# Second layer's expansion in a graph network: two engines evict, rings of eight groups, four pairs of PSUM banks

## The reference

```python
feat_n = feat * jax.lax.rsqrt(out_deg)[:, None]
h_src = feat_n[src]
copy_sum = jax.ops.segment_sum(h_src, dst, num_segments=N)
inner_sum = jax.ops.segment_sum(h_src * feat_n[dst], dst, num_segments=N)
rst = copy_sum @ weight1 + inner_sum @ weight2
...
rst = rst * jax.lax.rsqrt(in_deg)[:, None]
```

## Time and profile before

| | us |
|---|---|
| median of 3 runs | 19314.47 |
| lowest, highest run | 19310.16, 19331.81 |
| span of the profiled execution | 19335.7 |
| the expansion `ex2` in it, 13010 to 13755 | 745.0 |

### The profile page before, as it was taken

One profiled execution on the slowest core, in us unless ns is written; L12 is line 12 of the kernel. 1 busy time (PEld: TensorE's weight loads), 2 busy tenths in 40 slices (PEclk: granted clock), 3 DMA queues, 4 the chain that ended last, 5 costly groups with the idle time before them and its releaser, 6 DMA issues. The chain is left out here.

```text
span 19335.7 us, 330621 instructions
## 1 busy us (share of the span) xinstructions
PE 11298.7 (58%) x72558; PEld 8581.2 (44%) x72559; DVE 10446.0 (54%) x36907; ACT 4413.4 (23%) x11783; POOL 8860.6 (46%) x9490
## 2 busy tenths in 40 slices
PE   5555555555545666564475666656555665446886
PEld 4333333333324555554375444433224553225776
DVE  7655555555542333333464777772345445777776
ACT  0011111111101222221011342006201112445665
POOL 0456556556551555555674344530362444333332
PEclk9766766667665666666555566765555555557887
DMA  7622222222222222223233798757543776665554
GB/s 313 253 63 65 63 64 63 62 65 63 65 59 69 58 57 57 57 57 56 50 58 33 249 312 271 214 169 241 174 127 89 228 224 213 216 216 175 174 173 142
DMA packets 2143987, 2588.95 MB, mean 134 GB/s; under 512 B 892151, under 2 KB 1761472, under 8 KB 2143848
## 3 DMA queue, kind: packets, MB, share of 16 engines
q1 hardware_dynamic: 1755208, 1752.17, 31.5%
q0 software_dynamic: 353792, 654.90, 11.6%
q10 hardware_dynamic: 34848, 180.49, 2.3%
HBM read 1738.16 MB, written 848.30 MB: 134 GB/s over the span
## 5 line engine op out<-in xcount | busy, mean ns | idle before, releaser
L556 POOL DMA_INDIRECT edges_by_dst<-rec,pos x1568 | 1527.2, 974 | 2135.3 <-DVE rec L491 1694.2
L989 POOL DMA_INDIRECT sc_rows<-src_table,sc_idx x1664 | 1581.9, 951 | 1484.8 <-DVE sc_tp L1087 813.7
L556 POOL DMA_INDIRECT edges_by_cell<-rec,pos x1568 | 1532.7, 977 | 528.7 <-issue 528.4
L1734 PE MATMUL ex_rows<-table,ex_oh 128*128 x6528 | 1173.5, 348 | 821.1 <-DVE ex_oh L1702 423.8
L1820 PE MATMUL gs_part<-gs_rows,gs_oh 128*128 128x192 bf16 x6528 | 1100.8, 332 | 787.6 <-DVE gs_oh L1793 309.3
L1039 PE MATMUL sc_loc<-dst_table,sc_ohT 128*128 x3328 | 767.1, 403 | 1140.3 <-ACT sc_ohT L1005 1097.2
L1782 POOL DMA_INDIRECT gs_rows<-rows_by_src,chunk_read_by_src x1088 | 1059.9, 974 | 778.2 <-PE gs_part L1820 474.6
L2221 PE MATMUL at_part<-cell_edge_term,key_in_block 128*66 128x128 f32 x8704 | 1218.1, 304 | 252.4 <-issue 201.2
L1734 PEld LDWEIGHTS ex_rows<-table,ex_oh 128*128 128x128 bf16 x6528 | 752.1, 132 | 1242.2 <-issue 1202.7
L520 DVE SCALAR_TENSOR_TENSOR junk<-rowb,keycol,earlier 128x128 f32<-128x128 f32 (+1 forms) x3136 | 1151.4, 413 | 240.5 <-issue 236.3
L2221 PEld LDWEIGHTS at_part<-cell_edge_term,key_in_block 128*66 128x66 f32 x8704 | 1132.0, 158 | 323.5 <-issue 302.9
(11 more groups left out here) (393 smaller groups left out, 25910.8 us busy)
## 6 DMA issues: line engine op xcount, KB each, us to landing
ex_keys<-src_key_rows SPq DMA_DIRECT2D x1632, 128.0 KB
rows_by_src<-ex_stage SPq DMA_DIRECT2D x1088, 192.0 KB
rowb<-sort_key_rows SPq DMA_DIRECT2D x392, 512.0 KB
ex_keys<-dst_key_rows SPq DMA_DIRECT2D x1088, 128.0 KB
dst_rows_by_src<-patY ACTq DMA_DIRECT2D x1, 104448.0 KB
gs_rows<-dst_rows_by_src SPq DMA_DIRECT2D x544, 192.0 KB
scored_dst_rows_by_src<-patZ ACTq DMA_DIRECT2D x1, 71808.0 KB
scored_rows_by_src<-ex_stage SPq DMA_DIRECT2D x544, 132.0 KB
```

The source lines that it names most:

```text
L556: nc.gpsimd.indirect_dma_start(out=out, out_offset=bass.IndirectOffsetOnAxis(ap=pos[:, u, k, j:j + 1], axis=0), in_=row, in_offset=None).t ...
L989: nc.gpsimd.indirect_dma_start(out=rows[:, u, j, :], out_offset=None, in_=tabS, in_offset=bass.IndirectOffsetOnAxis(ap=idx[:, u, j:j + 1], ...
L1734: m = nc.tensor.matmul(rows[k][u % 2][r // 2][:, r % 2, 0:W], oh[k][:, u % 2, r * P:(r + 1) * P], t3[:, bass.ds(held[k][u], 1), :].rearran ...
```

## The change

`skewed` takes the ring's length as a parameter (default `RING`). The call `expand_rows(..., "ex2", t3, None, XB)` becomes `expand_source_rows(..., "ex2", t3, XB)`, a function of its own for the list by source. In it:

- `ring` is 8: rings of eight for key rows and for staged rows, a loop body of eight groups (68 bodies, 66 of them looped), key loads eight groups ahead.
- `deep` is 4: four pairs of PSUM banks.
- DVE evicts slots 0 and 1, ACT slots 2 and 3, each with a counter of its own; SP's store and PE's products wait for both.
- the counters have new names.

```diff
-def skewed(eng, n, stages, enter=None):
+def skewed(eng, n, stages, enter=None, ring=RING):
...
+def expand_source_rows(nc, counts, D, K, name, t3, toB):
+    W = 3 * C
+    ring, deep = 2 * RING, 4
+    n = D.NG // ring
...
+        keys = sb("keys", [P, ring, SLOTS * P], BF16)
+        oh = sb("oh", [P, 2, SLOTS * P], BF16)
+        stage = sb("stage", [P, ring, SLOTS, W], BF16)
+        rows = [[ctx.enter_context(nc.psum_tensor(f"{name}_rows{u}{h}", [P, 2, 256], F32)) for h in range(2)] for u in range(deep)]
+        s_key = [counts.get(f"source_keys_loaded{u}") for u in range(ring)]
+        s_out = [counts.get(f"source_rows_stored{u}") for u in range(ring)]
+        s_oh, s_mm, s_low, s_high = (counts.get(f"source_{x}") for x in ("onehots", "products", "low_slots_evicted", "high_slots_evicted"))
...
+                def load(i, u):
+                    g = i * ring + u
+                    wait(sp, s_oh, g - ring + 1)
+                    sp.nop(nofuse=True)
+                    sp.dma_start(keys[:, u, :], row_of(K.krB, g)).then_inc(s_key[u].sem, 16)
+
+                def store(i, u):
+                    g = i * ring + u
+                    wait(sp, s_low, g + 1)
+                    wait(sp, s_high, g + 1)
+                    sp.dma_start(toB[0:D.NCH, :].rearrange("(g p) c -> p g c", p=P)[:, bass.ds(g, 1), :].rearrange("p o c -> p (o c)"),
+                                 stage[:, u, :, :].rearrange("p r c -> p (r c)")).then_inc(s_out[u].sem, 16)
+                skewed(sp, n, [(ring, load), (-1, store)], ring=ring)
...
+                def turn(i, u):
+                    g = i * ring + u
+                    wait(dve, s_key[u], (i + 1) * 16)
+                    wait(dve, s_mm, g - 1)
+                    nc.vector.tensor_scalar(oh[:, u % 2, :], keys[:, u, :], K.iotac[:, :], None, ALU.is_equal).then_inc(s_oh.sem, 1)
+
+                def evict(i, u):
+                    g = i * ring + u
+                    wait(dve, s_mm, g + 1)
+                    wait(dve, s_out[u], i * 16)
+                    nc.vector.tensor_copy(stage[:, u, 0:2, :], rows[u % deep][0][:, :, 0:W]).then_inc(s_low.sem, 1)
+                skewed(dve, n, [(2, turn), (0, evict)], ring=ring)
...
+                    nc.scalar.copy(stage[:, u, 2:4, :], rows[u % deep][1][:, :, 0:W]).then_inc(s_high.sem, 1)
+                skewed(act, n, [(0, evict)], ring=ring)
...
+                def products(i, u):
+                    g = i * ring + u
+                    wait(pe, s_oh, g + 1)
+                    wait(pe, s_low, g - deep + 1)
+                    wait(pe, s_high, g - deep + 1)
...
-                expand_rows(nc, counts, D, K, "ex2", t3, None, XB)
+                expand_source_rows(nc, counts, D, K, "ex2", t3, XB)
```

More of the change, by code:

```diff
@@ L687, in step @@
                 continue
-            run(i + q // RING, q % RING)
+            run(i + q // ring, q % ring)
     for s in range(-first, 0):
-        step(0, s, 0, n * RING)
+        step(0, s, 0, n * ring)
     def body(i, last):
@@ L694, in body @@
             enter(i)
-        for u in range(RING):
-            step(i, u, 0 if isinstance(i, int) and i == 0 else None, RING if last else None)
+        for u in range(ring):
+            step(i, u, 0 if isinstance(i, int) and i == 0 else None, ring if last else None)
     loop(eng, n, body)
-    for s in range(RING, RING + lastly):
-        step(n - 1, s, None, RING)
+    for s in range(ring, ring + lastly):
+        step(n - 1, s, None, ring)
 class Count:
@@ L1744, in expand_rows, with sb, _, evict @@
             finished(*[(s, 16 * n) for s in s_key[k]], (s_oh[k], D.NG), (s_mm[k], D.NG), (s_ev[k], D.NG), *[(s, 16 * n) for s in s_out[k]])
+def expand_source_rows(nc, counts, D, K, name, t3, toB):
+    W = 3 * C
+    ring, deep = 2 * RING, 4
+    n = D.NG // ring
+    with ExitStack() as ctx:
+        def sb(nm, s, d):
+            return ctx.enter_context(nc.sbuf_tensor(f"{name}_{nm}", s, d))
+        keys = sb("keys", [P, ring, SLOTS * P], BF16)
[5 more added lines that the diff above has]
+        s_oh, s_mm, s_low, s_high = (counts.get(f"source_{x}") for x in ("onehots", "products", "low_slots_evicted", "high_slots_evicted"))
+        with nc.Block() as block:
+            @block.sync
+            def _(sp):
+                def load(i, u):
[10 more added lines that the diff above has]
+                skewed(sp, n, [(ring, load), (-1, store)], ring=ring)
+                for u in range(ring):
+                    wait(sp, s_out[u], n * 16)
+            @block.vector
+            def _(dve):
+                def turn(i, u):
[9 more added lines that the diff above has]
+                skewed(dve, n, [(2, turn), (0, evict)], ring=ring)
+            @block.scalar
+            def _(act):
+                def evict(i, u):
+                    g = i * ring + u
+                    wait(act, s_mm, g + 1)
+                    wait(act, s_out[u], i * 16)
+                    nc.scalar.copy(stage[:, u, 2:4, :], rows[u % deep][1][:, :, 0:W]).then_inc(s_high.sem, 1)
+                skewed(act, n, [(0, evict)], ring=ring)
+            @block.tensor
+            def _(pe):
+                held = {}
+                def products(i, u):
+                    g = i * ring + u
+                    wait(pe, s_oh, g + 1)
+                    wait(pe, s_low, g - deep + 1)
+                    wait(pe, s_high, g - deep + 1)
+                    for r in range(SLOTS):
+                        m = nc.tensor.matmul(rows[u % deep][r // 2][:, r % 2, 0:W], oh[:, u % 2, r * P:(r + 1) * P],
+                                             t3[:, bass.ds(held["b"][u], 1), :].rearrange("p o c -> p (o c)"), start=True, stop=True)
+                    m.then_inc(s_mm.sem, 1)
+                def blocks(i):
+                    held["b"] = nc.values_load_multi_w_load_instructions(K.cblk[0:1, 1, bass.ds(i * ring, ring)], engines=PE_ONLY,
+                                                                         min_val=0, max_val=D.blocks - 1, skip_runtime_bounds_check_because=CLAMPED)[1]
+                skewed(pe, n, [(0, products)], blocks, ring=ring)
+        finished(*[(s, 16 * n) for s in s_key + s_out], *[(s, D.NG) for s in (s_oh, s_mm, s_low, s_high)])
```

## The result

| | before | after |
|---|---|---|
| median, us (4 runs each) | 19323.14 | 19475.90 |
| lowest, highest | 19310.16, 19365.08 | 19471.08, 19477.98 |
| profiled execution: time, span | see above, 19335.7 | 19471.08, 19469.4 |

The ratio is 1.0074 [1.0062, 1.0086]. The forecast was 19314 with a range from 19280 to 19358, so the time is outside it and on the other side of "no change". The profiled execution of after has 1.7 us around its span; the spans differ by 133.7 us.

A forecast was written before the change was run, and what follows sets the result against it. SP's own instruction stream, issuing the DMAs, was taken to bound the expansion. Loop -4.3 us (second wait's +29.0 included) and head and tail +3.4 gave -0.9 us: 19314 us, range 19280 to 19358.

The forecast's parts named there:

- the change touches one stage only: Starting assumption: only the second layer's expansion, 745.0 us of a 19335.7 us span, is affected.
- the chance of slower, 11%: Chance of a slower whole, from a dearer SP wait and DVE as bound, less what stays within 0.2%.
- SP's wait: Rival in the expansion: the added store wait costs 130 ns, 40 us above forecast, 19354 us; 8%.
- VectorE as the bound of the expansion: Rival: DVE's one-hot, products and eviction don't overlap, 1.72 us a round, 190 us more, 19505 us; 4%.
- SP bounds the stage: Expansion: SP's own instruction stream sets the pace, 1.27 us a plain round; after, 10.94 us per eight-group body.
- The second wait: SP's added wait before each looped store: one EVENT_SEMAPHORE, 55 ns, 528 groups, +29.0 us.
- Bodies of eight: Expansion loop: 66 bodies for 134, each with 0.34 us beside its plain rounds, and eight fewer looped rounds.
- head and tail: Expansion's straight code around the loop: head 12.0 us, tail 8.0, together 20.0 against 16.6, +3.4 us.
- the 740 to 750: Sign for the forecast: the expansion takes 740 to 750 us after the change.
- Split and rings: Expansion: moving two evictions to DVE, rings of eight and four pairs of banks cost and gain nothing.
- didn't turn to products: Sign in the expansion: DVE's waits for keys turn into waits for products or slots.
- The first rival: Rings did bind: expansion falls to DMA's limit, 1.04 us a group, 566 us for 745, whole 19136; 7%.

The follow-up runs named there:

- experiment 2: The kernel before with 66 no-effect VectorE instructions ahead of the `attention_maxima` loop: 19195.67 us, ratio 1.0073 to before.
- experiment 1: After with 32 no-effect VectorE instructions ahead of the `attention_maxima` loop: 19055.04 us against before's 19059.37 on that chip, ratio 1.0002.
- experiment 5: After with 32 no-effect VectorE instructions, and one DMA for the keys or rows of two groups: 16387.42 us against before's 16674.25, ratio 0.9827.
- experiment 4: After with ScalarE evicting all four slots and stores waiting for one counter: 19033.28 us, ratio 0.9984 to before; expansion 700.5 us.
- experiment 6: After with rings of four, two pairs of banks, ScalarE evicting all slots and one counter for stores: 16684.23 us, one run; expansion 734.6 us.
- experiment 7: After with rings of four and two pairs of banks, eviction still split: 16685.04 us, one run; expansion 799.1 us.
- experiment 8: The kernel before with 64 no-effect VectorE instructions ahead of the `attention_maxima` loop: that stage 1417.9 us, one run.
- experiment 11: The kernel before with 56 no-effect VectorE instructions ahead of the `attention_maxima` loop: that stage 1404.7 us, one run.
- experiment 9: The kernel before with 48 no-effect VectorE instructions ahead of the `attention_maxima` loop and 16 more inside its body: that stage 1431.5 us, one run.
- experiment 12: After with one DMA for the keys or rows of two groups and ScalarE evicting all slots: 16414.64 us against before's 16686.01, one run.

## Why the prediction was wrong, step by step

**The step that failed: "the change touches one stage only".** I summed over the expansion and had no term for any other. Of what the change adds to VectorE's program I asked only what it costs where it runs. It also moves each later loop of that engine by 66 places, and one of them, 286 instructions long, came to reach over place 2576, into a fourth block. That term is +133 us in the traces; experiment 2 has it alone (ratio 1.0073), experiment 1 takes it away (1.0002). None of the rivals held this mechanism: the chance of slower, 11%, went to SP's wait and to VectorE as the bound of the expansion.

**SP bounds the stage: right.** SP had no wait at all in after's loop. Its key loads come with one longer gap per eight, here the last; the round before it is a shorter one of 1.23 us:

```profile
13402.80 0.34 SPq L1771 DMA_DIRECT2D ex_keys<-src_key_rows  x1
...
13404.03 0.34 SPq L1771 DMA_DIRECT2D ex_keys<-src_key_rows  x1
...
13405.60 0.34 SPq L1771 DMA_DIRECT2D ex_keys<-src_key_rows  x1
```

The body is 710.0 / 66 = 10.76 us for 10.94 predicted; a plain round 1.31 to 1.32 for 1.325 (the median distance in the loop is 1.315). Experiment 5 shows it from the other side.

**The second wait: right.** 55 ns were predicted as one EVENT_SEMAPHORE and no more ALU_OPs a store; it is 58 by experiments 4 and 1, and SP's instructions are those (duration at least, middle, most):

```profile
L745 SPq ALU_OP  x791: 32/33/36, 13029.9 to 13736.9; - x198
L745 SPq EVENT_SEMAPHORE  x527: 17/17/17, 13028.7 to 13737.0; - x176
L745 SPq FUSED_REGOPS  x132: 42/47/56, 13028.6 to 13730.3; - x132
L1777 SPq FUSED_REGOPS  x527: 37/37/51, 13028.7 to 13737.0; - x176
```

**A term that was missing in the stage: the new counters, -8.5 us.** I used that they start at zero only to say that both waits are for one value. It also takes an instruction out of SP's stream: one ALU_OP less a body of four in experiment 6. With the 38 ns of gap that the prediction reads from the earlier trace rows, 134 x (37 + 38) ns is 10 us, an estimate; 8.5 us were measured. That a value plus a base of zero needs no addition in one round of the four is my reading of it. In the kernels with bodies of eight single groups (after, experiments 1 and 4) an ALU_OP takes 33 ns and there are 12 a body, 1.5 a group for 1.25 before; experiment 6 has new counters and 37 ns, so the 33 aren't due to the counters, and their cause is open.

**Bodies of eight: right, a little small.** Predicted -33.3 and +3.4 for head and tail; experiments 6 to 4 give -34.1 for -29.9 (two chips; the expansion of the before versions differs by up to 3 us among them). The head took 12.2 us for 12.0, the tail 9.9 for 8.0. The stage in all: predicted -33.3 + 3.4 + 29.0 = -0.9; by the experiments -34.1 - 8.5 + 30.6 = -12.0, in the trace -13.4. So the stage's 732 us lie below the 740 to 750 that were written down.

**Split and rings "nothing, off the path": right for after, for half the reason.** DVE's eviction is 550 ns, as the earlier trace rows had it:

```profile
L1795 DVE CAST ex_stage<-ex_rows 128x384 bf16<-128x384 f32 x530 | 291.7, 550 | 0.0
```

Longer rings didn't end the waits. They moved them, in the loop's stretch:

```profile
ACT ex_stage L1804 <- DMA rows_by_src<-ex_stage: 403.7, 428, 1.9
...
DVE ex_oh L1789 <- DMA ex_keys<-src_key_rows: 227.1, 377, 1.6
```

ACT waits longer for its slots although it has twice as many, as foreseen. DVE waits less for keys, and its waits didn't turn to products, as I had put it (45 us, for 108 in the earlier trace rows); the 292 us that it now spends on evictions fill the time. But I priced split and rings as one edit. Apart from each other they are not free: with a ring of four the split puts DVE's eviction on the path (experiment 7, 64.5 us above experiment 6), which the rings of eight and the four pairs of banks then hide but for the wait itself.

**The first rival's floor holds for single transfers only.** It was put at 1.04 us a group by the first layer's 309 GB/s; with 1,024 bytes to a KB, as the trace counts them, 320 KB take 1.06. The DMA engines' own time before was 1.03, so for the change as it stood the floor was about right. In pairs, with key packets of 2 KB, it was 0.94 and 0.90, at 349 and 365 GB/s.

## What to carry to other kernels

When an edit adds or takes instructions on an engine, list that engine's later loops with their lengths: a long body, here of 286 and 302 instructions, can start to be read in anew at each turn, in a stage that the diff doesn't name. The signs are same busy times, idle time ended by issue right behind the branch, and packets on the instruction queue; instructions without effect ahead of the loop tell it apart at once. And where many engines wait for DMAs while the issuer waits for nothing, count the issuer's instructions: two groups to a DMA brought 1.7% (1.4% of it in the expansion), where rings and bodies twice as long brought 0.16% and a second evicting engine cost more than half of what they won in the stage.

## What the runs showed of the hardware

- A loop of 286 VectorE instructions has 0.22 to 0.24 us behind its branch back in some places of the program and 3.4 to 3.7 us (4.4 to 4.5 on other chips) in others, with about five packets of 8 KB a turn. The instructions at the places 2319 or 2320, 2448 and 2576 start 0.24 to 0.81 us later in the five slow kernels than in quick ones, the last by 0.35 us in each (after and experiments 2, 8 and 11; 9 with a loop of 302).
- A wait added to SP's stream costs 58 ns (experiments 4 and 1). SP's ALU_OP takes 33 ns in after, 1 and 4, and 37 in before and in 5, 6, 7 and 12, on the same line; the counters' age doesn't decide it.
- The DMA engines took 1.03 us a group at key packets of 1 KB (before) and 0.94 at 2 KB (experiment 5).
- TensorE's granted clock was 0.50 of full speed in the expansion while a group took 1.35 us (after), and 0.70 and 0.76 when it took 0.94 and 0.90 us (experiments 5 and 12). Matmul time fell with it, 441 to 355 and 322 us, off the path.
- Open: in experiments 5 and 7 the stage `attention_rows` took 1054 us for 1090 to 1092 in 6, 8 and 12, with a granted clock of 0.70 for 0.65 to 0.66. Of its cause no run here tells anything, and of experiment 5's gain of 287 us this may be some 37 (the expansion gives 232).
